# Eleven short groups of unread TensorE products in chunks 0, 14 and 15 of a Mamba block kernel

## The chip, the cores and the metric

One core of a Trainium2 chip runs the whole program. The metric is the device time of one execution in microseconds (us). Engines are named as in the profile: PE is TensorE (PEld its weight loads), DVE VectorE, ACT ScalarE, POOL GpSimd, SP the engine that issues DMAs.

## What is computed

The input x has 8 sequences of 1024 tokens with 256 features, all fp32. A layer norm is followed by a Mamba block and a residual, then a second layer norm, a feed-forward block with a shared expert (and routed experts, which the kernel computes only if a router weight reaches 1) and a residual. The part that matters here, cut from the reference:

```python
xz = einsum('bld,ed->ble', x, in_proj_w); xp, z = xz[..., :ED], xz[..., ED:]
xc = silu(conv1d(xp, conv_w))                       # 4 taps, causal
dt, Bm, Cm = split(einsum('ble,fe->blf', xc, x_proj_w))
delta = softplus(dt @ dt_proj_w.T + dt_proj_b)      # ED = 512
dA = exp(delta[..., None] * A)                      # N = 16 states
BX = delta[..., None] * Bm[:, :, None, :] * xc[..., None]
hs = associative_scan(h = dA * h + BX, axis=1)
y  = einsum('blen,bln->ble', hs, Cm) + D * xc
out = einsum('ble,de->bld', y * silu(z), out_proj_w)
```

## The kernel before

The 8192 tokens are cut into NQ = 16 chunks of 512 tokens (CH), two to a sequence. The 512 channels are G = 4 groups of 128 (a group is the partition axis of a tile), and the 16 states are taken Q = 2 at a time. So a chunk has S = 32 steps: step s of chunk c belongs to group s // 8 and to two of the states. Every engine has its own program, written out by hand, with one loop over chunks `c` and steps `s` (L464 for PE, L822 for ACT, L1118 for DVE, L1305 for POOL, L1416 for SP); in it, lists of conditions on `s` say which piece of the work of this or a neighbouring chunk is issued there. Semaphores join the engines.

The ring that each step passes through:

- PE, `pe_bx` (L222, products on L236): the input term BX of four states, 16 products, for **two** steps at once, at every odd step. Its tile BX takes four PSUM banks and there is one of it, so `e.wait_ge(s_scan, RT * m)` makes PE wait until the scans of the two steps before have read it.
- DVE, `dve_scan` (L940, scans on L950): two scans of 512 elements per step, which need BX and the decay `da` that ACT computes (L614). Between the scans DVE does the convolution taps (L981, L985), the gate (`dve_gate`, L1036, the multiply on L1041) and others.
- POOL, `pool_times_c` (L1228): multiplies the scanned states by C, which comes as `cb` by DMA.
- PE, `pe_sum` (L254, L260): adds the products of step k up in one of two PSUM banks Y[0], Y[1] by transposing products with the identity, two steps later. Group m = 4c + g uses bank Y[m % 2]; `dve_gate` reads it when the group is done and counts `s_gm`.

Around it PE does the projections: xp and z (`pe_xp` L296, `pe_z` L321), dBC (L330), dt (L346), transposes (L250, L337, L354, L362, L383, L401), the output product (L373, and L426 in the last chunk) and the feed-forward block (L393, L410, L418). The projections of chunk c+1 and c+2 and the output of chunk c-1 are issued in the steps of chunk c, so chunk 15, the last, has no projections to issue ahead, chunk 14 has fewer, and chunk 0 has no output of a chunk before. The convolution of chunks c+1 and c+2 borrows the free Y bank (`conv_bank`, L174) where such a chunk exists.

The order in a step of PE's loop is: the pieces of neighbouring chunks, then `pe_sum(e, k - 2)`, a transpose of gates at a few steps (`pe_yt`, L357), and last, at odd steps (L541), `pe_bx(e, (k + 1) // 2)`. PE runs in order: what stands before `pe_bx` runs while DVE scans, and if it is done early, PE idles until the scans are done.

The kernel has products that nobody reads at two places already: 24 and 3 of them (L439, L442) at the start, and `pe_warm` (L431, product on L434) after the last chunk. An fp32 product of this form shows as two rows of the trace, each with a weight load.

Of the kernel before, what the change touches and what calls it, by code (L numbers as in the profile page):

```python
# [10 lines left out]
P = 128  # L11
# [29 lines left out]
def mamba_moe(nc, x, in_wT, conv_w, x_wT, dt_wT, dt_b, A_log, D, out_wT, Ws1, Ws2, W1, W2, Wr, out):  # L41
# [7 lines left out]
    G = ED // P  # L49
# [3 lines left out]
    NQ = NB * HV  # L53
# [23 lines left out]
    with ExitStack() as ctx:  # L77
# [353 lines left out]
        def pe_warm(e, n):  # L431

            for _ in range(n):
                e.matmul(Y[1][:, 0:P], ident[:, :], ident[:, :], start=True, stop=True)  # L434

        def tensor(e):
            e.wait_ge(s_ident, 1)
            for _ in range(24):
                e.matmul(Y[1][:, 0:P], ident[:, :], ident[:, :], start=True, stop=True)  # L439
            pe_trc_first(e)  # L440
            for _ in range(3):
                e.matmul(Y[1][:, 0:P], ident[:, :], ident[:, :], start=True, stop=True)  # L442
            e.wait_ge(s_win, 16)
            for g in range(G):
                pe_xp_first(e, g)
            pe_z_first(e, 0)
            pe_z_first(e, 1)
            e.wait_ge(s_wt, 16 * 9)
            e.wait_ge(s_wdt, 2)
            e.wait_ge(s_const, 7)  # L450
            pe_dbc(e, 0, 0)
            pe_dbc(e, 0, 1)
            pe_z_first(e, 3, (0,))
            pe_dt(e, 0, 0)
            pe_bt(e, 0)
            pe_dt(e, 0, 1)
            pe_z_first(e, 3, (1,))
            pe_z_first(e, 2)
            pe_ut(e, 0, 0)
            e.wait_ge(s_d1_out, 1)  # L460
            pe_bx(e, 0)
            pe_trc(e, 1, 0)
            pe_trc(e, 1, 1)
            for c in range(NQ):  # L464
                for s in range(S):
                    k = S * c + s
                    if s == 2:
                        pe_ut(e, c, 1)
                    if s == 6:
                        pe_dt(e, c, 2)  # L470
                    if s == 16:
                        pe_dt(e, c, 3)
                    if s % NP == 2:
                        pe_skip(e, c, s // NP)
                    if s == 10:
                        pe_ut(e, c, 2)
                    if c == 0 and s in (0, 4, 8, 12):
                        pe_xp(e, G + s // 4)
                    if c and on(c + 1) and s in (4, 12):
                        pe_xp(e, G * c + s // NP + 6)  # L480
                    if s == 28 and on(c + 1):
                        pe_ut(e, c + 1, 0)
                    if on(c + 2) and s in (22, 28):
                        pe_xp(e, G * c + s // NP + 6)
                    if s == 0 and c:
                        pe_z(e, c, 3)
                    if s in (0, 2) and on(c - 2):
                        pe_shared(e, c - 2, s // 2)
                    if s == 2 and c and on(c + 2):
                        pe_trc(e, c + 2, 0)  # L490
                    if s in (12, 13) and c == 0:
                        pe_trc(e, 2, s - 12)
                    if on(c - 1):
                        if s == 4:
                            pe_yt(e, c - 1, 2)
                            pe_yt(e, c - 1, 3)
                        if s == 8:
                            pe_out(e, c - 1, 0)
                        if s == 9:
                            pe_out(e, c - 1, 1, 0, G // 2)  # L500
                        if s == 10:
                            pe_out(e, c - 1, 1, G // 2, G)
                        if s == 11:
                            pe_out(e, c - 1, 2, 0, G // 2)
                        if s == 13:
                            pe_out(e, c - 1, 2, G // 2, G)
                        if s == 14:
                            pe_out(e, c - 1, 3)
                    if on(c + 1):
                        if s == 7:  # L510
                            pe_z(e, c + 1, 0)
                        if s == 16:
                            pe_z(e, c + 1, 1)
                        if s in (18, 20):
                            pe_dbc(e, c + 1, s // 2 - 9)
                        if s == 22:
                            pe_bt(e, c + 1)
                    if s == 24 and on(c + 1):
                        pe_dt(e, c + 1, 0)
                    if s == 20:  # L520
                        pe_ut(e, c, 3)
                    if s in (26, 27) and on(c - 1):
                        pe_hidden(e, c - 1, s - 26)
                    if s == 29 and on(c - 1):
                        pe_htr(e, c - 1)
                    if s == 30 and on(c + 1):
                        pe_dt(e, c + 1, 1)
                        pe_z(e, c + 1, 2)
                    if k >= 2:
                        pe_sum(e, k - 2)  # L530
                    if s == 3 and c and on(c + 2):
                        pe_trc(e, c + 2, 1)
                    if s == 15:
                        pe_yt(e, c, 0)
                    if s == 21:
                        pe_yt(e, c, 1)
                    if s in (24, 25) and on(c - 1):
                        pe_otr(e, c - 1, s - 24)
                    if s == 30 and c == NQ - 1:
                        pe_yt(e, c, 2)  # L540
                    if s % 2 and 0 <= k + 1 < S * NQ:  # L541
                        pe_bx(e, (k + 1) // 2)

            e.wait_ge(s_pa_out, len(a_use))
            e.wait_ge(s_pb_out, len(b_use))
            e.wait_ge(s_gm, G * NQ - 1)
            pe_shared_prev(e, 0)
            pe_out_last(e, 0, range(G - 1))
            pe_sum(e, S * NQ - 2)
            pe_out_last(e, 1, (0,))  # L550
            pe_sum(e, S * NQ - 1)
            pe_out_last(e, 1, (1,))
            e.wait_ge(s_gm, G * NQ)
            for t in range(TB):
                mm = e.transpose(BX[:, t * P:(t + 1) * P], gate[(NQ - 1) % 2][:, t, (G - 1) * P:G * P], ident[:, :])
            mm.then_inc(e_yt, 1)
            pe_out_last(e, 1, (2,))
            for h in range(2):
                e.wait_ge(e_yt_out, h + 1)
                pe_out_last(e, h, (G - 1,))  # L560
            pe_shared_prev(e, 1)
            pe_warm(e, 12)
            for h in range(2):
                if h:
                    pe_warm(e, 2)
                e.wait_ge(e_xn, h + 1)
                for kk in range(KD):
                    for t in (2 * h, 2 * h + 1):
                        lo = (2 + h) * CH + kk * CH // 2 + (t % 2) * P
                        mm = e.transpose(BX[:, lo:lo + P], x2n[:, t, kk * P:(kk + 1) * P], ident[:, :])  # L570
                mm.then_inc(e_tr, 1)
            for h in range(2):
                e.wait_ge(e_tr_out, h + 1)
                e.wait_ge(e_sp_out, 2)
                for t2 in range(2):
                    t = 2 * h + t2
                    lo = h * CH + t2 * (F + NE)
                    for kk in range(KD):
                        mm = e.matmul(BX[:, lo:lo + F + NE], x2T[:, kk, t * P:(t + 1) * P], w_hr[:, kk, :],
                                      start=(kk == 0), stop=(kk == KD - 1))  # L580
                mm.then_inc(e_hl, 1)
            for h in range(2):
                e.wait_ge(e_relu, h + 1)
                for t2 in range(2):
                    lo = (2 + h) * CH + t2 * P
                    mm = e.transpose(BX[:, lo:lo + P], h_tok[:, 2 * h + t2, :], ident[:, :])
                mm.then_inc(e_ht, 1)
            for h in range(2):
                e.wait_ge(e_ht_out, h + 1)
                e.wait_ge(e_res, h + 1)  # L590
                for t2 in range(2):
                    t = 2 * h + t2
                    mm = e.matmul((PA, PB)[h][:, t2 * DM:(t2 + 1) * DM], hT[:, t * P:(t + 1) * P], w_s2[:, :], start=True,
                                  stop=True)
                mm.then_inc(e_sh, 1)
            e.wait_ge(s_any, 1)
            e.matmul(Y[0][0:1, 0:1], any_p[:, :], ones[:, :], start=True, stop=True).then_inc(s_any, 1)
# [979 lines left out]
```

## Time and profile before

| | |
|---|---|
| time, median of 3 runs | 1572.64 us (1570.89 to 1573.24) |
| the profiled execution | 1570.26 us |
| its span, first to last instruction | 1568.1 us |
| busy PE / DVE / ACT / POOL | 92% / 94% / 80% / 90% |
| mean granted TensorE clock | 0.993 |
| PE waiting for DVE's scans, before `pe_bx` | 91.4 us in 186 waits, the longest 2.5 us |

The profiled execution is one; its span leaves out 2.2 us of its own time, and its time is 2.4 us under the median. In a timeline each row is a run of like instructions: start, length, engine, line, operation, tiles, count, and in square brackets how long the engine sat idle before it and which engine released it. Rows overlap a little, since products are pipelined. The granted clock is a share of full speed: 1.00 is 2.4 GHz and 0.50 is 1.2 GHz.

### The profile page before, as it was taken

The page shows a single profiled execution, that of the slowest core. Times are in us where ns is not written, and L with a number is a line of the kernel's source. Part 1 is how long each engine was busy: PE and PEld are TensorE (multiplying, and loading weights), DVE is VectorE, ACT ScalarE, POOL GpSimd, SP SyncE. Part 2 cuts the span into 40 slices and gives each one's busy share as a digit, 9 for nine tenths or more (in the row PEclk, how much of TensorE's full clock was granted, in tenths as well). Part 3 has the DMA queues.
Part 4 walks back from the last instruction along what each step waited for, and adds up shares of the span by engine and source line. Part 5 has one row for each costly group of instructions (what it writes and reads, how often), then busy time and mean ns, then how long its engine had stood idle before and what let it go on. Part 6 is the DMA issues. An engine that isn't in the chain of part 4 may idle for free.

```text
span 1568.1 us, 39429 instructions
## 1 busy us (share of the span) xinstructions
PE 1448.2 (92%) x15188; PEld 1124.8 (72%) x15188; DVE 1474.4 (94%) x1773; ACT 1257.9 (80%) x2100; POOL 1410.3 (90%) x1248
## 2 busy tenths in 40 slices
PE   8889999999999999999999999999999999998887
PEld 5666777676776777777777776777777776776776
DVE  6999999999999999999999999999999999998885
ACT  7887887887888888887887888888887887787761
POOL 2899999999999999999999989999998999999993
PEclk9999999999999999999999999999999999999999
DMA  5103032040402204031040402204031030402201
GB/s 155 65 3 136 2 97 69 7 158 3 136 29 69 96 3 162 2 100 65 13 152 3 136 28 71 95 3 162 2 102 63 13 139 3 150 2 70 95 15 42
DMA packets 78514, 106.49 MB, mean 68 GB/s; under 512 B 42289, under 2 KB 67761, under 8 KB 70130
## 3 DMA queue, kind: packets, MB, share of 16 engines
q1 hardware_dynamic: 78322, 103.92, 20.7%
q8 instruction: 122, 2.00, 0.5%
q14 instruction: 70, 0.57, 0.1%
HBM read 86.10 MB, written 17.30 MB: 66 GB/s over the span
## 4 chain that ended last, share of the span: by engine, by line
DVE 31%; PE 20%; ACT 19%; issue 15%; POOL 10%; DMA 2%; SPq 1%; DVEq 1%; ACTq 0%; POOLq 0%
DVE hs L950 27%; PE BX L236 9%; ACT da L614 8%; POOL hs L1238 8%; PE Y L296 4%; PE Y L260 3%; DMA cb<-c_scratch 1%; ACT xc L681 1%; ACT x2n L751 1%; PE PB L346 1%; SPq L1367 1%; DVE st L962 1%; ACT xp L649 1%; ACT u L719 1%; DVE Y L981 1%
## 5 line engine op out<-in xcount | busy, mean ns | idle before, releaser
L1238 POOL TENSOR_TENSOR hs<-hs,cb 128x1024 f32<-128x1024 f32 x512 | 1210.4, 2365 | 67.2 <-DVE hs L950 45.2
L950 DVE TENSOR_TENSOR_SCAN hs<-da,BX 128x512 f32<-128x512 f32 x1024 | 1165.5, 1201 | 59.8 <-PE BX L236 50.5
L614 ACT ACTIVATE da<-delta,a_neg 128x511 f32<-128x511 f32 (+1 forms) x1024 | 663.6, 711 | 24.9 <-DVE hs L950 24.4
L260 PEld LDWEIGHTS Y<-ident,hs 128*128 128x128 f32 x4096 | 467.4, 141 | 92.9 <-issue 62.5
L260 PE MATMUL Y<-ident,hs 128*128 128x128 f32 x4096 | 514.0, 274 | 8.5 <-POOL hs L1238 8.5
L236 PE MATMUL BX<-bd,uT 32*128 32x128 f32 x8192 | 303.1, 285 | 96.6 <-DVE hs L950 91.4
L236 PEld LDWEIGHTS BX<-bd,uT 32*128 32x128 f32 x8192 | 253.7, 187 | 157.3 <-DVE hs L950 155.0
L296 PE MATMUL Y<-xnT,w_in 128*128 128x512 f32 x240 | 119.5, 621 | 0.9 <-ACT xnT L630 0.9
L649 ACT ACTIVATE xp<-Y 128x512 f32<-128x512 f32 x60 | 35.9, 598 | 101.2 <-PE Y L296 100.7
L321 PE MATMUL PA<-w_in,xnT 128*128 128x512 f32 x240 | 114.5, 599 | 0.0
L981 DVE SCALAR_TENSOR_TENSOR Y<-xp,w_conv,Y 128x512 f32<-128x512 f32 x120 | 88.9, 741 | 2.6 <-ACT Y L651 0.9
L1256 POOL TENSOR_TENSOR u<-delta,xc 128x512 f32<-128x512 f32 x64 | 81.7, 1276 | 3.6 <-DVE delta L1019 3.6
L1234 POOL COPY hlast<-hs 128x2 f32<-128x2 f32 x256 | 47.6, 186 | 40.8 <-DVE hs L950 39.2
L717 ACT ACTIVATE u<-PB 128x512 f32<-128x512 f32 x63 | 37.5, 596 | 49.2 <-PE PB L346 47.4
L321 PEld LDWEIGHTS PA<-w_in,xnT 128*128 128x128 f32 x240 | 43.1, 190 | 45.0 <-issue 43.1
L346 PE MATMUL PB<-dbc,w_dt 97*128 97x512 f32 x126 | 71.6, 650 | 0.0
L296 PEld LDWEIGHTS Y<-xnT,w_in 128*128 128x128 f32 x240 | 41.6, 193 | 37.3 <-issue 31.0
L734 ACT ACTIVATE uT<-PB 128x512 f32<-128x512 f32 x48 | 28.6, 597 | 49.0 <-PE PB L354 49.0
L330 PE MATMUL PA<-xc,w_x 128*96 128x512 f32 x128 | 61.4, 602 | 0.9 <-ACT xc L663 0.9
L373 PE MATMUL PB<-w_out,ygT 128*128 128x256 f32 x240 | 60.8, 386 | 0.9
L373 PE MATMUL PA<-w_out,ygT 128*128 128x256 f32 x240 | 60.8, 386 | 0.0
L1248 POOL TENSOR_TENSOR da<-first,hlast 128x2 f32<-128x2 f32 x256 | 51.2, 200 | 0.0
(186 smaller groups left out, 1496.9 us busy)
## 6 DMA issues: line engine op xcount, KB each, us to landing
cb<-c_scratch SPq DMA_DIRECT2D x64, 1024.0 KB, 4.8
x<-in_x SPq DMA_DIRECT2D x16, 512.0 KB, 4.0
x_scratch<-x2T SPq DMA_DIRECT2D x16, 512.0 KB, 6.6
xt<-in_x SPq DMA_DIRECT2D x15, 512.0 KB, 4.9
bd<-bt SPq DMA_DIRECT2D x480, 1.0 KB
out<-x SPq DMA_DIRECT2D x15, 512.0 KB, 3.2
w_in<-in_in_wT SPq DMA_DIRECT2D x1, 1024.0 KB, 8.3
c_scratch<-dbc SPq DMA_DIRECT2D x64, 8.0 KB, 1.5
```

The costliest lines, as they stand in the source:

```text
L236: mm = e.matmul(BX[:, q * CH + j * P:q * CH + (j + 1) * P], uT[rows, g, j, :], bd[rows, (NR * c + p) % BR, j, :, :].rearrange("p t n -> p ...
L260: mm = e.matmul(Y[(G * c + g) % 2][:, t * P:(t + 1) * P], hs[:, k % HR, q, t * P:(t + 1) * P], ident[:, :], is_transpose=True, start=False ...
L296: mm = e.matmul(bank[:, :], w_in[:, kk, g * P:(g + 1) * P], xnT[c % 2][:, kk, :], start=(kk == 0), stop=(kk == KD - 1))
L321: mm = e.matmul(bank[:, :], xnT[c % 2][:, kk, t * P:(t + 1) * P], w_in[:, kk, ED:2 * ED], start=(kk == 0), stop=(kk == KD - 1))
L330: mm = e.matmul(PA[0:FX, :], w_x[:, g, :], xc[:, (G * c + g) % XR, :], start=(g == 0), stop=(g == G - 1))
L346: e.matmul(bank[:, :], w_dt[:, g * P:(g + 1) * P], dbc[:, :].rearrange("f (j q t) -> f q j t", j=J, q=RT), start=True, stop=True).then_inc ...
L373: mm = e.matmul(bank[:, t2 * DM:(t2 + 1) * DM], ygT[:, g, t * P:(t + 1) * P], w_out[:, g, :], start=(g == 0), stop=(g == G - 1))
L614: e.activation(da[:, k % DR, q, h:], delta[:, g, h:], ACT.Exp, scale=a_neg[:, g, n:n + 1]).then_inc(s_da, 1)
L950: e.tensor_tensor_scan(hs[:, k % HR, q, :], da[:, k % DR, q, :], BX[:, :].rearrange("p (t n) -> p n t", n=RT)[:, n % RT, :], float(c % HV) ...
L981: e.scalar_tensor_tensor(out=bank[:, :], in0=xp[:, g, kk:kk + CH], scalar=w_conv[:, g, kk:kk + 1], in1=bank[:, :], op0=ALU.mult, op1=ALU.a ...
L1238: e.tensor_tensor(hs[:, k % HR, :, :], hs[:, k % HR, :, :], cb[:, Q * p:Q * p + Q, :], ALU.mult).then_inc(s_hc, 1)
L1256: e.tensor_tensor(u[:, m % UR, :].rearrange("p (j q t) -> p q j t", j=J, q=RT), delta[:, g, :].rearrange("p (q j t) -> p q j t", j=J, q=RT ...
```

## The change

At eleven odd steps PE issues 4 to 6 products of the identity with itself just before `pe_bx`, 128 columns each. In chunk 0 (steps 25 and 27) they go to the PSUM bank PA, after a wait for the release of the use before it. In chunk 14 (steps 23 and 29) and chunk 15 (steps 5, 7, 13, 17, 21, 23 and 29) a new function `pe_fill` writes them to the Y bank that the current group does not use, after a wait until that bank's last gate has been read. Their results are overwritten by the next product with `start=True`. In all 60 products, 120 rows of the trace.

```diff
+        def pe_fill(e, c, s, n):
+
+            m = G * c + (s - 2) // NP
+            e.wait_ge(s_gm, m)
+            for _ in range(n):
+                e.matmul(Y[(m + 1) % 2][:, 0:P], ident[:, :], ident[:, :], start=True, stop=True)
...
                     if s == 30 and c == NQ - 1:
                         pe_yt(e, c, 2)
+                    if c == 0 and s in (25, 27):
+
+                        e.wait_ge(*released("bt", 1, 0))
+                        for _ in range(5):
+                            e.matmul(PA[:, 0:P], ident[:, :], ident[:, :], start=True, stop=True)
+                    if c == NQ - 2 and s in (23, 29):
+                        pe_fill(e, c, s, 5)
+                    if c == NQ - 1 and s in (5, 7, 13, 17, 21, 23, 29):
+                        pe_fill(e, c, s, 4 if s == 21 else 6)
                     if s % 2 and 0 <= k + 1 < S * NQ:
                         pe_bx(e, (k + 1) // 2)
```

No other engine's program changes. On PE, steps 24 to 28 of chunk 0 (L552 is the new product, L236 `pe_bx`, L260 `pe_sum`, L250 the first product of a new group, L354 a transpose of u for the next chunk):

```order
 L346 MATMUL PB<-dbc,w_dt 128x512
 L260 MATMUL Y<-ident,hs 128x128 x16
-L236 MATMUL BX<-bd,uT 128x128 x16
-L250 MATMUL Y<-ident,xc 128x128 x4
-L260 MATMUL Y<-ident,hs 128x128 x16
+L552 MATMUL PA<-ident 128x128 x5
+L236 MATMUL BX<-bd,uT 128x128 x16
+L250 MATMUL Y<-ident,xc 128x128 x4
+L260 MATMUL Y<-ident,hs 128x128 x16
+L552 MATMUL PA<-ident 128x128 x5
 L236 MATMUL BX<-bd,uT 128x128 x16
 L354 MATMUL PB<-ident,u 128x128 x4
```

Five products stand before each of the two `pe_bx`; the rest keeps its order. On PE, steps 22 to 24 of chunk 14 (L441 is the product in `pe_fill`, L337 the transpose of B for chunk 15):

```order
 L337 MATMUL PA<-ident,dbc 128x96 x4
 L260 MATMUL Y<-ident,hs 128x128 x16
+L441 MATMUL Y<-ident 128x128 x5
 L236 MATMUL BX<-bd,uT 128x128 x16
 L346 MATMUL PB<-dbc,w_dt 128x512
```

Again only the five products are new. On PE, step 29 of chunk 15, the last `pe_bx` of the program:

```order
 L401 MATMUL PB<-ident,x2n 128x128 x4
 L260 MATMUL Y<-ident,hs 128x128 x8
+L441 MATMUL Y<-ident 128x128 x6
 L236 MATMUL BX<-bd,uT 128x128 x16
 L260 MATMUL Y<-ident,hs 128x128 x8
```

Six products now stand before it.

## Rows read from the trace of the kernel before

**Rows 1.** The page: busy time of each engine, share of the span, instructions.

```profile
PE 1448.2 (92%) x15188; PEld 1124.8 (72%) x15188; DVE 1474.4 (94%) x1773; ACT 1257.9 (80%) x2100; POOL 1410.3 (90%) x1248
```

**Rows 2.** PE's waits in 60 to 160, 160 to 1376, 1376 to 1545 us.

```profile
PE BX L236 <- DVE hs L950: 10.9, 13, 1.8
...
PE BX L236 <- DVE hs L950: 54.4, 145, 1.0
...
PE BX L236 <- DVE hs L950: 22.6, 25, 2.1
```

**Rows 3.** Windows: length, each engine's busy us, granted clock (PEclk), DMA share, GB/s.

```profile
119.30:122.70 3.40, 3.40 (x26) 2.28 (x23) 2.36 (x3) 0.60 (x1) 3.32 (x3) 0.51 0.06 4
1423.10:1426.50 3.40, 3.40 (x34) 2.45 (x35) 1.33 (x2) 2.03 (x4) 3.32 (x3) 0.50 0.06 2
1501.70:1505.10 3.40, 3.40 (x18) 3.40 (x17) 3.40 (x4) 1.80 (x4) 3.40 (x4) 0.51 0.00 0
1518.70:1522.10 3.40, 3.40 (x27) 3.18 (x20) 2.95 (x3) 1.03 (x3) 3.09 (x4) 0.50 0.01 2
1535.70:1539.10 3.40, 3.40 (x41) 3.17 (x38) 1.79 (x3) 0.00 (x0) 2.20 (x1) 0.51 0.03 5
...
160.00:1376.00 1216.00, 1150.52 (x12210) 892.93 (x12208) 1182.56 (x1417) 1010.94 (x1691) 1134.94 (x990) 1.00 0.22 69
```

**Rows 4.** Timeline of PE, steps 25 to 29 of chunk 0.

```profile
112.82 1.17 PE L236 MATMUL BX<-bd,uT 32*128 32x128 f32 x32 [1.76 <-DVE hs L950]
...
118.67 1.62 PE L236 MATMUL BX<-bd,uT 32*128 32x128 f32 x32 [1.72 <-DVE hs L950]
...
125.45 1.17 PE L236 MATMUL BX<-bd,uT 32*128 32x128 f32 x32
```

**Rows 5.** Timeline of PE, steps 23, 25 and 29 of chunk 14.

```profile
1423.05 2.07 PE L236 MATMUL BX<-bd,uT 32*128 32x128 f32 x32 [1.71 <-DVE hs L950]
...
1429.77 1.17 PE L236 MATMUL BX<-bd,uT 32*128 32x128 f32 x32 [0.22 <-DVE hs L950]
...
1441.74 1.17 PE L236 MATMUL BX<-bd,uT 32*128 32x128 f32 x32 [1.45 <-DVE hs L950]
```

**Rows 6.** Timeline of PE, step 5 and steps 17 to 29 of chunk 15.

```profile
1465.14 1.17 PE L236 MATMUL BX<-bd,uT 32*128 32x128 f32 x32 [1.91 <-DVE hs L950]
...
1500.24 1.17 PE L236 MATMUL BX<-bd,uT 32*128 32x128 f32 x32 [1.87 <-DVE hs L950]
...
1502.02 3.39 PE L260 MATMUL Y<-ident,hs 128*128 128x128 f32 x16
1506.09 1.17 PE L236 MATMUL BX<-bd,uT 32*128 32x128 f32 x32 [0.68 <-DVE hs L950]
...
1511.94 1.17 PE L236 MATMUL BX<-bd,uT 32*128 32x128 f32 x32 [1.33 <-DVE hs L950]
...
1517.79 1.31 PE L236 MATMUL BX<-bd,uT 32*128 32x128 f32 x32 [2.08 <-DVE hs L950]
...
1523.75 1.18 PE L236 MATMUL BX<-bd,uT 32*128 32x128 f32 x32 [0.40 <-DVE hs L950]
...
1535.45 1.86 PE L236 MATMUL BX<-bd,uT 32*128 32x128 f32 x32 [2.09 <-DVE hs L950]
1537.24 1.97 PE L260 MATMUL Y<-ident,hs 128*128 128x128 f32 x8
...
1539.53 1.04 PE L260 MATMUL Y<-ident,hs 128*128 128x128 f32 x8
...
1545.70 1.04 PE L260 MATMUL Y<-ident,hs 128*128 128x128 f32 x8
```

**Rows 7.** Timeline of DVE and of POOL in the tail.

```profile
1546.77 0.69 DVE L1041 TENSOR_TENSOR gate<-gate,Y 128x512 f32<-128x512 f32 x1 [0.99 <-PE Y L260]
...
1542.23 2.35 POOL L1238 TENSOR_TENSOR hs<-hs,cb 128x1024 f32<-128x1024 f32 x1
```

**Rows 8.** Timeline of PE, the unread products that the kernel has after the last chunk.

```profile
1551.46 2.84 PE L434 MATMUL Y<-ident 128*128 128x128 f32 x24
```

## The prediction

> **What bounds the kernel now.** I read the page's busy shares first. DVE is busy 94% of the span, PE 92%, POOL 90% [rows 1]. No engine is idle enough for time to be won by moving work, so the question is which engine waits for which. In PE's waits there is one large entry: the product BX waits for DVE's scans. In the middle of the program (160 to 1376 us) it is 54.4 us over 145 waits and never longer than 1.0 us; in 169 us at the end it is 22.6 us over 25 waits, the longest 2.1 us, and early, in 60 to 160 us, 10.9 us over 13 [rows 2]. The long waits therefore stand exactly in the chunks that the change touches.
>
> In those stretches the bound is the ring of one BX tile: product BX (1.17 us), four scans, product BX again. Its beat can be read off the starts of BX: 1500.24 to 1506.09 and 1506.09 to 1511.94 are 5.85 us each [rows 6]. PE's other work lies under the scans, and what is left of it is the wait. So more work for PE costs nothing there as long as it fits in the wait.
>
> Then I looked at the granted clock in small windows. After such waits it falls from 1.00 to 0.50, that is from 2.4 to 1.2 GHz. It does so near five of the places that the change fills: 119.3 to 122.7, 1423.1 to 1426.5, 1501.7 to 1505.1, 1518.7 to 1522.1 and 1535.7 to 1539.1 us [rows 3]. Before each fall PE had waited 1.7 to 2.1 us for the scans, with little but transposes and the small products of BX around the wait.
>
> **What the falls cost.** A product at half clock takes about twice as long, but only what the ring or the end of the program waits for counts. I compare the distance of two starts of BX with the 5.85 us of the beat.
>
> - 119.3: BX starts at 118.67 and takes 1.62 us, then come products at half speed, and the next BX starts at 125.45 with no wait in front of it, so PE was the late one [rows 4]. The distance is 6.78 us, and the price is **0.93 us**. PE does 1.7 us less in the low stretch, so it would be done at 123.75, before the ring's 124.52: the 0.93 comes back whole.
> - 1423.1: BX takes 2.07 us instead of 1.17, the next one starts at 1429.77, 6.72 us later, after a wait of 0.22 [rows 5]. Price **0.87 us**.
> - 1501.7: BX at 1500.24 was through; 16 transposes take 3.39 us, but the next BX at 1506.09 still waits 0.68 us for the scans and keeps the beat [rows 6]. Price **0**.
> - 1518.7: BX takes 1.31 us, the distance to 1523.75 is 5.96 us [rows 6]. Price **0.1 us**.
> - 1535.7: the last BX takes 1.86 us, 0.69 too long; behind it there is no ring but PE's own tail. The eight transposes at 1537.24 take 1.97 us where the same eight at 1539.53 take 1.04 [rows 6]. All 3.4 us of the low stretch lie on PE's path, so up to 1.7 us come back. What could hold them up is POOL's last multiplication, which ends at 1544.58 and follows the scans, so it comes only 0.69 us earlier, at 1543.9; the sum that needs it stands at 1545.70, and 1.7 us earlier is 1544.0 [rows 6, 7]. DVE's gate waits for that sum (0.99 us, [rows 7]). So I take **1.6 us**.
>
> Sum 0.93 + 0.87 + 0 + 0.1 + 1.6 = 3.5 us. The ring passes on what is gained earlier: POOL idles for DVE later on, and the waits in the middle are few tenths, so an earlier end of chunk 0 only moves all that follows.
>
> **What the change adds.** 60 products, 120 rows. The same product in the tail shows 24 rows in 2.84 us [rows 8], that is 0.12 us a row. Ten rows (5 products) take 1.2 us, twelve 1.4 us, eight 0.95 us. The waits that they go into: 1.76 and 1.72 us in chunk 0 [rows 4], 1.71 and 1.45 in chunk 14 [rows 5], and 1.91, 1.87, 1.33 (the one with 4 products), 2.08 and 2.09 at steps 5, 17, 21, 23 and 29 of chunk 15 [rows 6]; those at steps 7 and 13 are like step 5. The tightest are 1.2 in 1.45 and 0.95 in 1.33. At full clock all fit, and I cost them at nothing. The cover is the scans: where a wait were gone, a group would cost its 1.2 to 1.4 us. The added waits of PE are for things that are over by then: the gate of the group before is issued on DVE two steps ahead, and the transposed B was copied by ACT at step 22 of chunk 0. Queued behind them are BX and through it the scans, so a late one would show at once; I count 0, and at most a tenth each. A write of PE into Y or PA while DVE scans BX is nothing new, since the transposes into Y run under the scans all the time.
>
> What a fill does to the clock is not in this trace. Between the bounds that it takes away no fall (gain 0) and all five (3.5 us), I take nearly all of them, for the nearest rows speak for it: a fill leaves at most 0.7 us of each wait open, and between 160 and 1376 us, where no wait is longer than 1.0 us, the mean granted clock is 1.00 [rows 2, 3].
>
> There is one more doubt, about which falls another execution has. The wait of 1.91 us before 1465.14 brought no fall here, one of 1.87 before 1500.24 did [rows 6]. So the length of the wait does not decide alone, and another execution may fall at other places, with other prices: 0 where BX is through before, 0.9 where all of it is slow, 1.7 in the tail. Five falls at the mean of the prices above are 3.5 us; if the tail is spared in about half of the executions, some 2.7. Since the executions timed are others than the profiled one, I take **3.0 us**. The profiled execution would come to 1570.26 - 3.0 = 1567.3 us; the median stands 2.4 us above it and I leave that distance, so 1572.64 - 3.0 = **1569.6 us**.
>
> The measured clock sets what a fall costs; a page would set it higher. The Trainium skill, in "TensorE: Matmul & The Clock Gate", section "HAM oscillation — how this bites in real kernels", reckons the penalty as the throttled time times (1 - 1.2/2.4). By that, an estimate from the five stretches of 3.4 us, the change would bring 8.5 us and the time would be 1564.1. The trace disagrees at 1501.7, where a whole low stretch moved BX by nothing.
>
> **The rivals.**
>
> - *All half-clock time comes back.* 5 x 3.4 us at half speed are 8.5 us, so 1564.1. For it: PE is busy in every one of the low stretches [rows 3]. Against it: the waits behind them, 0.68 and 0.40 us [rows 6], which take up the slowness. Chance 0.04.
> - *The falls only move.* The fills keep the clock up for one wait, and it falls after another that isn't filled, or a fill is too thin. Gain and loss cancel: 1572.6. For it: falls come after waits of equal length in one place and not in another. Against it: the unfilled waits next to them are 0.68 and 0.40 us [rows 6]. Chance 0.14.
> - *Slower: fills that run at half clock.* Eight transposes take 1.97 us at half clock against 1.04 [rows 6], so a row then takes twice its 0.12 us, and twelve 2.8 us. That is 0.9 us more than a wait of 1.9, and BX and the scans behind it start 0.9 us late. It decides from the point where the clock is low when a fill starts. If that is so at five places it costs 4.5 us, and with the falls remaining the time is 1577.1. Against it: each fall begins at or after BX, not in the wait, so the fill would still run at full clock, and the low stretch is over before the next filled wait. Chance 0.05.
> - *The change does nothing to the clock, since these falls belong to the profiled execution alone.* Then the time stays at 1572.6. Three runs within 2.3 us of each other can't exclude it. Chance 0.04.
>
> **How the numbers follow.** My forecast, falls gone and a gain of 1 to 4.8 us around 3.0, has 0.73. A measurement of this kernel can tell about 0.2% from no change, which is 3.1 us: the forecast lies at that line, and I give 0.37 of its 0.73 to faster and 0.36 to the same. With the first rival faster is 0.41; with the second and the fourth the same is 0.54; slower is 0.05. The range 1567.4 to 1572.4 takes in gains from 0.2 to 5.2 us; it leaves out the first and the third rival and part of the second.
>
> **What the profile after would show.** The granted clock at 1.00 at all places of [rows 3], moved by the gain. The waits of BX in chunks 0, 14 and 15 shrink by 0.9 to 1.4 us at the eleven places while starts of BX keep 5.85 us. The last BX takes 1.17 us, and the tail from it to the gate is shorter by about 1.6 us. The prediction is wrong if a fill is followed by BX with no wait in front of it and a beat above 5.85 (fills too long), if low stretches show up at unfilled waits, or if the falls are gone and the starts of BX have not moved (the ring was not what set the end).

## The result and the profile after

The change took 1566.16 us (median of 6 runs, 1565.86 to 1567.01) against 1571.87 us before (6 runs, 1567.69 to 1573.24). The ratio is 0.9967, 95% interval 0.9957 to 0.9978: 5.2 us less, where 3.0 were forecast and 1569.6 us. The time lies below the range that was given. Two more comparisons later gave 0.9968 (0.9956 to 0.9980) and 0.9974 (0.9964 to 0.9983). Over all runs of this study the kernel before has a median of 1570.89 us (119 runs, 1567.47 to 1574.92) and the change 1566.80 us (21 runs, 1565.82 to 1568.17). So the gain is 4 to 5 us, and the spread shrank from 7.5 to 2.4 us (from 7.4 us in 23 runs to 1.3 us in 6 where both ran side by side).

The profiled execution took 1566.09 us, its span is 1564.0. Busy shares first, from its page; they answer to [rows 1].

```profile
PE 1452.4 (93%) x15308; PEld 1129.9 (72%) x15308; DVE 1474.4 (94%) x1773; ACT 1258.2 (80%) x2100; POOL 1410.5 (90%) x1248
```

PE has 120 rows more and 4.2 us more of busy time, and the program is shorter. DVE's busy time is the same to the digit. PE's waits for the scans in 60 to 160, 160 to 1376 and 1376 to 1545 us answer to [rows 2]:

```profile
PE BX L236 <- DVE hs L966: 8.0, 12, 1.6
...
PE BX L236 <- DVE hs L966: 54.7, 147, 1.0
...
PE BX L236 <- DVE hs L966: 13.0, 24, 2.1
```

In the last stretch the wait went from 22.6 to 13.0 us, in the middle it did not change. The windows of the same stretches (length, busy us of each engine, granted clock, DMA share, GB/s):

```profile
60.00:160.00 100.00, 87.83 (x952) 66.80 (x956) 92.74 (x97) 82.25 (x132) 92.37 (x80) 1.00 0.16 54
160.00:1376.00 1216.00, 1150.28 (x12226) 892.92 (x12224) 1182.57 (x1417) 1010.89 (x1692) 1135.04 (x992) 1.00 0.21 69
1376.00:1545.00 169.00, 152.43 (x1718) 128.67 (x1714) 149.12 (x166) 112.47 (x185) 152.38 (x129) 1.00 0.13 42
```

None of the five low stretches of [rows 3] is there: the clock is 1.00 in all three. The timeline of PE at the places of [rows 4, 5, 6]:

```profile
110.42 1.28 PE L552 MATMUL PA<-ident 128*128 128x128 f32 x10
112.35 1.17 PE L236 MATMUL BX<-bd,uT 32*128 32x128 f32 x32 [0.65 <-DVE hs L966]
...
118.20 1.17 PE L236 MATMUL BX<-bd,uT 32*128 32x128 f32 x32 [0.59 <-DVE hs L966]
...
123.34 1.09 PE L260 MATMUL Y<-ident,hs 128*128 128x128 f32 x8 [0.80 <-POOL hs L1254]
124.37 1.17 PE L236 MATMUL BX<-bd,uT 32*128 32x128 f32 x32
...
1421.99 1.17 PE L236 MATMUL BX<-bd,uT 32*128 32x128 f32 x32 [0.59 <-DVE hs L966]
...
1427.84 1.17 PE L236 MATMUL BX<-bd,uT 32*128 32x128 f32 x32 [0.38 <-DVE hs L966]
...
1433.69 1.17 PE L236 MATMUL BX<-bd,uT 32*128 32x128 f32 x32 [0.49 <-DVE hs L966]
...
1438.42 1.28 PE L441 MATMUL Y<-ident 128*128 128x128 f32 x10
1439.63 1.17 PE L236 MATMUL BX<-bd,uT 32*128 32x128 f32 x32
...
1498.12 1.17 PE L236 MATMUL BX<-bd,uT 32*128 32x128 f32 x32 [0.53 <-DVE hs L966]
...
1503.97 1.17 PE L236 MATMUL BX<-bd,uT 32*128 32x128 f32 x32 [2.06 <-DVE hs L966]
...
1515.67 1.17 PE L236 MATMUL BX<-bd,uT 32*128 32x128 f32 x32 [0.73 <-DVE hs L966]
...
1521.52 1.17 PE L236 MATMUL BX<-bd,uT 32*128 32x128 f32 x32 [0.94 <-DVE hs L966]
...
1530.97 1.50 PE L441 MATMUL Y<-ident 128*128 128x128 f32 x12
1533.22 1.17 PE L236 MATMUL BX<-bd,uT 32*128 32x128 f32 x32 [0.75 <-DVE hs L966]
1534.33 1.09 PE L260 MATMUL Y<-ident,hs 128*128 128x128 f32 x8
...
1543.69 0.66 PE L571 MATMUL BX<-ident,gate 128*128 128x128 f32 x4
```

Every BX takes 1.17 us. The fills lie in the waits, and at ten of the eleven places 0.4 to 0.8 us of the wait is left. Three things in these rows were not foreseen. In chunk 0 the distance from 118.20 to 124.37 is 6.17 us and not the beat of 5.85: with PE no longer late, its sums wait 0.80 us for POOL. At step 29 of chunk 14 the sum waits for POOL first, the fill starts late, and BX at 1439.63 has no wait in front: 5.94 us since 1433.69, so that fill costs 0.09 us. The 1.45 us that stood there in [rows 5] were themselves the work of a fall: the ring had just been held back at 1423.1, which gave POOL time to catch up (the sum waits 0.20 us for it there). A later execution of the kernel before without that fall (1567.96 us, below) has a sum that waits 0.73 us for POOL and only 0.93 us of wait before BX, less than the 1.28 us of the five products. And step 19 of chunk 15, which is not filled, has a wait of 2.06 us (BX at 1503.97). In [rows 6] it was 0.68 only because PE was slow before it.

**Where the time went in the profiled pair.** Between the same two points of the program, in us:

| from | to | before | after |
|---|---|---|---|
| BX at step 3 of chunk 0 | BX at step 5 of chunk 0 | 6.40 | 5.85 |
| BX at step 25 of chunk 0 | BX at step 29 of chunk 0 | 12.63 | 12.02 |
| BX at step 29 of chunk 0 | BX at step 23 of chunk 14 | 1297.60 | 1297.62 |
| BX at step 23 of chunk 14 | BX at step 29 of chunk 15 | 112.40 | 111.23 |
| BX at step 29 of chunk 15 | last transposes of gates | 12.06 | 10.47 |
| last transposes of gates | end of the span | 20.58 | 20.28 |

At the filled places that makes 0.61 + 1.17 + 1.59 = 3.37 us of the 4.1 us of span. 0.55 us is a fall near 47 us that no fill of the change reaches, and that this execution of the changed kernel happened not to have. 0.30 us is at the end.

### The profile page after: what moved, and what is told of

The parts are those of the page before. It is cut to its first block, busy times and chain, and to the rows that moved or that the text cites. A ratio compares the mean times of both kernels' runs of the same rounds, so it can differ in the third digit from the quotient of the medians.

```text
span 1564.0 us, 39669 instructions
## 1 busy us (share of the span) xinstructions
PE 1452.4 (93%) x15308; PEld 1129.9 (72%) x15308; DVE 1474.4 (94%) x1773; ACT 1258.2 (80%) x2100; POOL 1410.5 (90%) x1248
## 4 chain that ended last, share of the span: by engine, by line
DVE 30%; ACT 19%; PE 18%; issue 16%; POOL 11%; DMA 2%; SPq 2%; DVEq 1%; ACTq 0%; POOLq 0%
DVE hs L966 26%; POOL hs L1254 9%; PE BX L236 8%; ACT da L630 8%; PE Y L296 4%; SPq L1383 2%; DMA cb<-c_scratch 2%; PE Y L260 2%; ACT xc L697 1%; ACT xp L665 1%; PE PB L346 1%; ACT x2n L767 1%; ACT u L735 1%; DVE st L978 1%; DVE Y L997 1%
## 5 line engine op out<-in xcount | busy, mean ns | idle before, releaser
L260 PEld LDWEIGHTS Y<-ident,hs 128*128 128x128 f32 x4096 | 463.7, 141 | 96.5 <-issue 61.5
L260 PE MATMUL Y<-ident,hs 128*128 128x128 f32 x4096 | 511.5, 273 | 11.3 <-POOL hs L1254 11.2
L236 PE MATMUL BX<-bd,uT 32*128 32x128 f32 x8192 | 300.4, 283 | 85.3 <-DVE hs L966 80.3
L236 PEld LDWEIGHTS BX<-bd,uT 32*128 32x128 f32 x8192 | 251.6, 186 | 145.4 <-DVE hs L966 143.0
```

The costliest lines, as they stand in the source:

```text
L236: mm = e.matmul(BX[:, q * CH + j * P:q * CH + (j + 1) * P], uT[rows, g, j, :], bd[rows, (NR * c + p) % BR, j, :, :].rearrange("p t n -> p ...
L260: mm = e.matmul(Y[(G * c + g) % 2][:, t * P:(t + 1) * P], hs[:, k % HR, q, t * P:(t + 1) * P], ident[:, :], is_transpose=True, start=False ...
```

## The experiments

Two theories stood against each other. **A**: an execution's falls are not always the same; those of most other executions of the kernel before cost more than the profiled one's, and the fills take away any of them. **B**: the executions differ in something else (DMA, the start), each place gives what it gave in the profiled pair, and the first comparison had a costly draw.

**The kernel before, twice more.** No edit.

> The kernel before, unchanged, so that more of its executions show their time beside their mean granted clock. Theory A (the executions differ in which waits bring a fall of TensorE's clock, and the falls of the slower ones cost more than the 3.5 us that the profiled execution shows): 1567 to 1574 us, the time rises as the mean clock falls from about 0.996 to 0.991, and the profile shows falls at other waits of chunks 0, 14 and 15 than those of the profiled execution. Theory B (the executions differ in something else, DMA arrival or the start): the same spread of times at one and the same clock of 0.993.

> One more look at the kernel before, for where its falls are and what each costs by the distance of two starts of BX. Theory A: falls at some of 47, 112 to 119, 1423, 1441, 1465 to 1500, 1518 and 1536 us, prices from 0 to 1.9 us whose sum, added to 1565.6, gives the execution's time within 0.7 us.

Measured: 1570.69 us (12 runs, ratio 1.0001), and one execution of 1567.96 us. Each run lists its time and its mean granted clock. The medians by clock, over 113 runs of the kernel before from four comparisons:

```
clock   0.989    0.990    0.991    0.992    0.993    0.994    0.995    0.996
runs        7       15       21       24       14       12       15        4
us    1573.51  1572.80  1572.25  1570.65  1570.57  1570.27  1567.92  1568.56
```

One more run has 0.997 and 1568.34 us. A line through the 113 points has 0.80 us for each 0.001 of clock and reaches 1565.6 us at 0.999, near the change's own fastest runs. B, which had the same spread at one and the same clock, falls. The profiles show the falls in other places too: the first of the two has them near 49, 114, 1424, 1465, 1520 and 1537 us, the second near 114, 1500, 1517 and 1534 us. (Each of the 17 profiles of this study has one low stretch more, which begins behind PE's last product. It delays no product, but it counts in the mean clock.)

**Only the waits, no products.**

```diff
-                        for _ in range(5):
-                            e.matmul(PA[:, 0:P], ident[:, :], ident[:, :], start=True, stop=True)
-                    if c == NQ - 2 and s in (23, 29):
-                        pe_fill(e, c, s, 5)
-                    if c == NQ - 1 and s in (5, 7, 13, 17, 21, 23, 29):
-                        pe_fill(e, c, s, 4 if s == 21 else 6)
+                    if c == NQ - 2 and s in (23, 29) or c == NQ - 1 and s in (5, 7, 13, 17, 21, 23, 29):
+                        e.wait_ge(s_gm, G * c + (s - 2) // NP)
```

> Only the added semaphore waits, no product. Both theories: the waits are for things long over, so 1570.5 and the spread of the kernel before. A time below 1569 would mean that the gain comes from the order of the waits and not from the clock.

Measured 1571.52 us, ratio 0.9996 (0.9986 to 1.0007): no gain. The products do it, not the order. The bare waits are not quite free: in its profile, where no fall interferes, BX behind them comes 0.03 to 0.09 us later than in the kernel before (in chunk 15 5.88 to 5.94 us after the BX before it, in place of 5.85). Behind the fills of the change this lateness does not show. The profiled execution was the longest of those profiled, 1574.56 us at clock 0.990, and shows what a fall can cost. Timeline of PE and one window of it, steps 29 and 31 of chunk 14:

```profile
1442.17 1.87 PE L236 MATMUL BX<-bd,uT 32*128 32x128 f32 x32 [1.08 <-DVE hs L961]
1443.97 2.06 PE L346 MATMUL PB<-dbc,w_dt 97*128 97x512 f32 x2
1445.84 1.91 PE L321 MATMUL PA<-w_in,xnT 128*128 128x512 f32 x4
1447.58 1.91 PE L260 MATMUL Y<-ident,hs 128*128 128x128 f32 x16
1449.42 1.17 PE L236 MATMUL BX<-bd,uT 32*128 32x128 f32 x32
...
1442.30:1445.70 3.40, 3.40 (x34) 2.29 (x35) 1.68 (x3) 0.00 (x0) 3.00 (x5) 0.52 0.97 300
```

The distance is 7.25 us, 1.40 over the beat. Here both ends of the fall count: BX itself is slow, and behind it stands so much work of PE (dt, z and the sums) that PE comes too late for the next BX. In the profiled execution of before this place had no fall. The same form at step 7 of chunk 15 (1472.90 to 1480.17) costs 1.42 us. Against the undisturbed distances of the changed kernel, the four executions without fills carry:

```
execution (us)                       1570.26  1570.75  1574.56  1567.96
near 47 us (not filled)                 0.55     0.60     1.87     0.00
chunk 0, steps 25 to 29                 0.61     0.08     0.36     0.00
chunk 14 step 23 to chunk 15 step 29    1.17     2.01     4.06     0.00
tail, from the last BX                  1.59     1.50     1.55     1.59
time less these                      1566.34  1566.56  1566.72  1566.37
```

The first column is the profiled execution of before; the third still has the added waits in it, about 0.5 us of its 4.06. (In the fourth column two differences of -0.01 and -0.08 are put at 0.) What is left is the same within 0.4 us, and 0.3 to 0.6 us above the 1566.09 of the changed kernel. In these profiles A covers the spread and all but that rest of the gain. Its sum was to start from 1565.6 us and come within 0.7 us; from there it is 0.7 to 1.1 us short, so that start was too low.

**One chunk at a time.** Each keeps the fills of one chunk; for chunk 15 alone:

```diff
-                    if c == 0 and s in (25, 27):
...
-                    if c == NQ - 2 and s in (23, 29):
-                        pe_fill(e, c, s, 5)
```

> Only the seven fills of chunk 15. Theory A (most of the gain is in chunk 15 and the tail, since most long waits and the 1.7 us of the tail are there): 1567.8 to 1569, two thirds of the 5.2 us. Theory B (the gain is a constant of each place as priced in the profiled execution: 1.7 us in chunk 15): 1570.2.

> Only the two fills of chunk 14. Theory A: a fall in about a third to a half of the executions at 0.9 us, so 0.3 to 0.5 us, 1571.4. Theory B: 0.9 us less in each, 1571.0.

> Only the two fills of chunk 0. The profiled pair shows 0.6 us at this place, not the 0.93 of the prediction, since the sums wait for POOL once PE is no longer late. Theory A: 0.3 to 0.6 us, 1571.4. Theory B: 0.6 us in each, 1571.3. Over 1.5 us would mean that something else in chunk 0 gains.

Measured: only chunk 15 1569.36 us, ratio 0.9984 (0.9975 to 0.9992), between what A and B expected; only chunk 14 1570.36, ratio 0.9993 (0.9985 to 1.0002); only chunk 0 1571.89, ratio 1.0004 (0.9994 to 1.0015). So only chunk 15 by itself is clear, about 2.5 us by the ratio and 1.2 us by the medians, and the mean clock of its runs is 0.9956 against 0.9920 of the 35 runs of the kernel before beside it. The other two are not resolved: 11 runs out of a spread of 6 us do not measure half a microsecond. By the ratios the three add up to 3.0 us and the whole gives 4 to 5; with these intervals that is no contradiction, and no proof of a sum either.

What the times leave open, the three profiles show. (Falls near 48 us, which no fill here reaches, are left out.) With chunk 0 filled there is no fall between steps 25 and 29 of chunk 0, but there are falls at 1423.6, 1471.4, 1502.1 and 1519.2 us. With chunk 14 filled there is none in chunk 14, but at 113.0 and from 1464.7 to 1536.4 us five more. With chunk 15 filled there is one in chunk 14, at 1421.4, and one behind the unfilled step 19 of chunk 15. In none of the profiles of this study does a fall begin at a filled wait. The one at 1421.4 is the dearest in all profiles; its low stretch lasts 6.8 us where most last 3.4. Timeline of PE in that profile, steps 23 and 25 of chunk 14, and two windows:

```profile
1421.81 2.09 PE L236 MATMUL BX<-bd,uT 32*128 32x128 f32 x32 [1.70 <-DVE hs L959]
...
1429.69 1.17 PE L236 MATMUL BX<-bd,uT 32*128 32x128 f32 x32
...
1421.40:1424.80 3.40, 2.99 (x33) 2.30 (x34) 1.19 (x2) 2.51 (x5) 3.32 (x3) 0.50 0.06 2
1424.80:1428.20 3.40, 3.40 (x14) 2.73 (x13) 3.40 (x4) 0.00 (x0) 2.64 (x3) 0.50 0.06 2
```

This distance is 7.88 us and the next one 6.41, together 2.59 us over two beats.

The profile with only chunk 0 filled is the one without a fall in the tail. Timeline of PE:

```profile
1536.80 1.17 PE L236 MATMUL BX<-bd,uT 32*128 32x128 f32 x32 [2.08 <-DVE hs L962]
1537.90 1.09 PE L260 MATMUL Y<-ident,hs 128*128 128x128 f32 x8
```

The wait of 2.08 us is there, and the tail takes 10.46 us as in the changed kernel. In the six other profiles whose last wait isn't filled it takes 11.97 to 12.06.

**All fills but the last.**

```diff
-                    if c == NQ - 1 and s in (5, 7, 13, 17, 21, 23, 29):
+                    if c == NQ - 1 and s in (5, 7, 13, 17, 21, 23):
```

> All fills but the six products before the last BX (step 29 of chunk 15). Theory A (the tail's fall costs up to 1.6 us, and comes in about half of the executions): two levels, one near 1566.2 and one near 1567.8, median between them. Theory B (the tail's fall comes always when its wait is not filled): 1567.8 in all.

Measured 1567.62 us (1566.98 to 1569.25), ratio 0.9977 (0.9968 to 0.9986), against 0.9968 for the change beside it. The fastest of its 12 runs is 1.0 us above the fastest of the change's 6. The tail's fall is worth about 1 us in the mean. That the fastest runs are so far apart speaks for a fall in nearly every execution, but only the profiled one shows it; the two levels that A expected did not show.

**The change again, and transposes in place of products.**

```diff
-                e.matmul(Y[(m + 1) % 2][:, 0:P], ident[:, :], ident[:, :], start=True, stop=True)
+                e.transpose(Y[(m + 1) % 2][:, 0:P], ident[:, :], ident[:, :])
```

with twice the count (10 for 5, 12 for 6, 8 for 4), and the same in PA.

> The change as it is, again beside the kernel before, so that both are compared over more executions. Theory A (the fills take away whatever falls an execution has): 1565.8 to 1567, median 1566.2, spread about 1 us, against 1570.5 before with a spread of 6 us; ratio 0.997 to 0.9975. Theory B (the first comparison had a costly draw of the kernel before and the change is worth the 3.0 us that were forecast): ratio 0.998.

> Every fill product replaced by two transposes of the identity, so that PE has as many rows of work in the same waits, but only transposes. If any work of the engine counts for the clock: 1566.2 as with the change. If transposes do not count (a page of the Trainium skill, TensorE: Matmul & The Clock Gate, Part 4, says that a transpose does not count as busy in the same way): the falls are back, 1570 to 1571, clock 0.992 to 0.996.

Measured: the change 1567.02 us (1565.98 to 1567.30), the transposes 1566.96 us (1565.98 to 1567.79), both ratio 0.9968, and a mean clock of 0.9972 in both. One fill of transposes and the BX behind it, from PE's timeline:

```profile
1461.24 1.47 PE L441 MATMUL Y<-ident 128*128 128x128 f32 x12
1463.31 1.17 PE L236 MATMUL BX<-bd,uT 32*128 32x128 f32 x32 [0.60 <-DVE hs L966]
```

Twelve transposes last as long as six products (1.47 and 1.50 us) and keep the clock as well. The Trainium skill, in "TensorE: Matmul & The Clock Gate", section "Part 4: PE-mode transpose", says that transposes do not count as busy in the same way. If they counted for nothing, the time would have been that of the kernel before, 4 us more; the trace disagrees with that. Whether they count in full no run shows, since two products in place of four to six do nearly as well (below).

Both profiles have one fall left in chunk 15, and one near 48 us, in chunk 0, which no fill of the change reaches. PE's timeline of the change's second profile, steps 19 to 21, and a window of it:

```profile
1504.22 1.17 PE L236 MATMUL BX<-bd,uT 32*128 32x128 f32 x32 [2.06 <-DVE hs L966]
1505.33 1.11 PE L354 MATMUL PB<-ident,u 128*128 128x128 f32 x4
1506.23 3.12 PE L260 MATMUL Y<-ident,hs 128*128 128x128 f32 x16
1509.19 0.60 PE L362 MATMUL PB<-ident,gate 128*128 128x128 f32 x4
1509.62 1.06 PE L441 MATMUL Y<-ident 128*128 128x128 f32 x8
1510.61 1.17 PE L236 MATMUL BX<-bd,uT 32*128 32x128 f32 x32
...
1505.30:1508.70 3.40, 3.40 (x20) 3.38 (x17) 3.35 (x4) 2.22 (x4) 2.86 (x3) 0.50 0.00 0
```

The fall is behind the wait of step 19, which the change leaves open. The work that it slows eats the next wait, the fill of step 21 then runs on into the time of BX, and the distance is 6.39 us, 0.54 too long. Without the fill PE would have been free at about 1509.7, before the ring's 1510.07, so by these rows the 0.54 us are the fill's own; no run has tried that pair alone. This is not the slower rival of the prediction: the low stretch is over when the fill starts, and its 8 rows take 1.06 us, full speed. PE was late, and the fill has lost its cover.

**Thinner and longer fills.** Two products everywhere, and all counts doubled; the lines of chunk 15:

```diff
-                        pe_fill(e, c, s, 4 if s == 21 else 6)
+                        pe_fill(e, c, s, 2)
```

```diff
-                        pe_fill(e, c, s, 4 if s == 21 else 6)
+                        pe_fill(e, c, s, 8 if s == 21 else 12)
```

> Every fill cut to two products (0.45 us of work instead of 0.9 to 1.4 us). If falls are decided by how much PE has done around the wait, some places fall below and some do not: between 1567 and 1571, say 1568.5, clock 0.994 to 0.998. If any product in the wait is enough: 1566.5 as with the change.

> Every fill doubled (8 to 12 products, 1.8 to 2.7 us). The clock stays at full, but the cover is gone: each fill overruns its wait of 1.3 to 2.1 us by 0.4 to 0.9 us, eleven places, so 5 to 8 us over the change: 1572 to 1574.5, with a spread as narrow as that of the change. If the ring had slack beyond the wait, it would stay near 1566.5.

Measured: two products 1566.87 us (1566.55 to 1568.20), ratio 0.9978 (0.9969 to 0.9987), mean clock 0.9970. That is no different from the change in its last comparison (0.9974). The expectation of 1568.5 was wrong: over the eleven places together 0.45 us of work in a wait is nearly enough. At step 29 of chunk 14, where five products cost 0.09 us, two leave a wait of 0.48 us and cost nothing. Doubled: 1572.67 us, ratio 1.0014 (1.0005 to 1.0023), mean clock 0.9974. PE's timeline, step 7 of chunk 15:

```profile
1469.57 2.84 PE L441 MATMUL Y<-ident 128*128 128x128 f32 x24
1472.34 1.17 PE L236 MATMUL BX<-bd,uT 32*128 32x128 f32 x32
```

The clock is as good as with the change, but no wait is left before BX, and the distance from 1465.75 is 6.59 us. The cover gone, the fills cost about 6 us over the change, which lies in the expected 5 to 8. Not all of it is plain overrun: in this profile there is again a fall behind the unfilled step 19, and step 21 comes 1.42 us late.

**More fills.** In chunk 0 at steps 3, 9, 11 and 15; at step 19 of chunk 15; and both.

```diff
+                    if c == 0 and s in (3, 9, 11, 15):
+                        e.wait_ge(*released(*{3: ("trc", 1, 1), 9: ("dt", 0, 2), 11: ("dt", 0, 2), 15: ("trc", 2, 0)}[s]))
+                        for _ in range({3: 6, 9: 3, 11: 5, 15: 4}[s]):
+                            e.matmul((PB if s in (9, 11) else PA)[:, 0:P], ident[:, :], ident[:, :], start=True, stop=True)
...
+                    if c == NQ - 1 and s == 19:
+                        e.wait_ge(*released("res", c - 1, 1))
+                        for _ in range(6):
+                            e.matmul(PA[:, 0:P], ident[:, :], ident[:, :], start=True, stop=True)
```

> The change and four more fills in chunk 0, at steps 3, 9, 11 and 15, where PE waits 2.5, 1.0, 1.6 and 1.3 us for the scans and where two executions of the kernel before fell near 47 us at a price of 0.5 and 1.9 us. Theory A: the falls near 47 and 67 us are gone too, 1565.8 to 1566.3, 0.5 us less than the change in the median. If the fills overrun (step 15 has 4 products in 1.3 us): at most 0.2 us more than the change.

> The change and one more fill, at step 19 of chunk 15 into the bank PA. Two profiles with the change's fills have their only fall behind that wait of 2.06 us, with a distance of 6.39 us to the next BX in place of 5.85. If the fill takes that fall away: the executions of the change near 1567.0 move to 1566.4, the median 0.3 to 0.5 us below the change's in the same comparison. If the fall only moves again: the same as the change.

> The change, the fill at step 19 of chunk 15 and the four more of chunk 0. If every fall that is left belongs to a wait that is not filled: 1565.8 to 1566.3, clock 0.999 in all executions and a spread under 0.5 us. If falls come from something that fills don't reach: clock 0.997 to 0.999 and a spread of 1 us as before.

> The change itself, to compare the two others with on one chip. 1565.8 to 1567.3, median 1566.4 to 1567.0, clock 0.997 to 0.999.

Measured: chunk 0 alone 1566.80 us (11 runs, 1565.89 to 1567.15), no gain that shows, where 1565.8 to 1566.3 was expected; beside each other step 19 alone 1566.27 us (8 runs, 1565.86 to 1567.65), both 1565.78 us (6 runs, 1565.50 to 1566.54) and the change 1566.80 us (9 runs, 1565.82 to 1568.17). The two profiles of which the expectation for step 19 speaks have a fall near 48 us too, so the one behind step 19 was not their only one; the profile with the fill at step 19 has the one near 48 us alone, and that with both fills has none. With both, no run has a clock under 0.999, against 0.996 to 0.999 for the change, and the median is 1.0 us lower. Its spread is 1.04 us where less than 0.5 was expected, so not all of the spread is the clock's. That is the best version. Against the kernel before its ratio is 0.9967 (0.9954 to 0.9980) where the change has 0.9974 (0.9964 to 0.9983); the intervals overlap, and the 1.0 us rests on medians of 6 and 9 runs. Its profiled execution (1565.57 us) has its last BX at 1533.22 us, as the first profile of the change has, and is 0.5 us shorter only behind the last transposes of gates.

## Why the prediction was wrong in size

The mechanism held; two terms of the sum were mis-sized. The forecast of 1569.6 us missed the 1566.16 us by 3.5 us, outside the range. Over all runs of the study, 1.75 us of this are the starting point, a median of three runs at 1572.64 where 119 give 1570.89; 1.1 us are the gain, 3.0 where the medians give 4.1; and 0.6 us are luck of the six runs of the change, 1566.16 where 21 give 1566.80. In detail:

- *The ring with a beat of 5.85 us, and PE's work free as long as it fits the wait*: right. The beat is there after the change in nearly all steps, and doubling the fills cost about what their overrun says.
- *The fills cost nothing*: right but for 0.09 us at step 29 of chunk 14, where POOL delays the sum before the fill and the wait is 0.93 us and not 1.45 once no fall comes before it, and for the 0.54 us at step 21 of chunk 15 where a fall stands ahead.
- *The falls go*: right in the profiled execution, all five.
- *Their prices*, 0.93 + 0.87 + 0 + 0.1 + 1.6 = 3.5 us: the sum held (3.37 us), its parts less so. Chunk 0 gave 0.61, since the undisturbed distance is 6.17 us there, not 5.85: POOL was next. The fall at 1423.1 cost 1.14 and not 0.87, since the step behind it was late by another 0.27 us ([rows 5]: 1429.77; the next BX before came 6.12 us later, now 5.85). The tail gave 1.59, as worked out.
- *"If the tail is spared in about half of the executions, some 2.7"* and the 3.0 us taken from it: **the step that failed first**. The tail fell in six of seven profiles without its fill, and elsewhere a fall costs up to 1.4 us where work stands behind it, and 1.9 (near 47 us) and 2.6 us (at 1421.4) where the low stretch is twice as long. The text had 0.9 as the most outside the tail.
- *"The median stands 2.4 us above it and I leave that distance"*: **the step that failed worst**. The 2.4 us were mostly the draw of three runs: over 119 the median of before stands 0.6 us above the profiled execution, over 21 that of the change 0.7 us above its own. As the times by clock show, such a draw is in the main a draw of falls, and the fills take them away. From the profiled execution the sum gives 1570.26 - 3.5 = 1566.8 us, which is the change's median over its 21 runs.
- *All half-clock time comes back*, 8.5 us: too much. Over the runs of before, 0.001 of clock is 1568 x 0.002 = 3.1 us at half clock and cost 0.80 us, a quarter. The Trainium skill, in "TensorE: Matmul & The Clock Gate", section "HAM oscillation — how this bites in real kernels", reckons half of it. (The low stretch at the end, which costs nothing, blurs this figure.)
- *The falls only move*: in part. One did, to step 19, in two of the change's three profiles. Against this rival stood the wait of 0.68 us there, which a fall had shortened; undisturbed it is 2.06 us.
- *Slower, fills at half clock*: not seen. In no profile does a low stretch reach into a fill; the 0.54 us at step 21 are a fill at full clock behind a late PE.
- *Faster, same or slower*: the likeliest was put at 0.54 for no difference; a gain of 0.33% is beyond the 0.2% line. The steps above made it so: 4 to 5 us stand clear of that line of 3.1 us, and 3.0 did not.

Two of the prediction's own signs of being wrong did show: a fill with no wait behind it (step 29 of chunk 14), and low stretches at an unfilled wait (step 19 of chunk 15).

Open: the stretch between the last transposes of gates and the end of the span, which is 19.8 to 20.7 us long in the profiles and whose scatter no fill explains, though it is nearly as large as what sets the best version apart; and the split of the gain among chunks 0 and 14.

## What to carry to other kernels

When PE waits in a ring that another engine bounds, look at the granted clock right behind its longest waits; a few unread products in the wait, well shorter than it, keep the clock, and nothing is lost as long as a wait remains in front of the next product that others need. Price a fall by the distance between two starts on the ring against the undisturbed distance of the same steps, and look at several executions: one profile shows one draw. If a kernel's times scatter with the mean clock, a median of few runs is a draw of falls (here 1.75 us off with three runs): take more runs before a sum starts from it. And a wait read from a trace with falls may be longer or shorter than the undisturbed one (1.45 and 0.93 us, 0.68 and 2.06 us here).

## What was not expected of the hardware

The same wait brings a fall in one execution and none in the next: 1.91 us before step 5 of chunk 15 had none at 1465.14 [rows 6] and one in the second execution; the tail's 2.08 us had none once in seven. Transposes of the identity kept the clock as well as products did (1566.96 and 1567.02 us). And two products, about 0.45 us, in waits of 1.3 to 2.1 us did nearly as much as four to six (1566.87 and 1566.80 us).
